# Head tiles: scaling one tile later, two output buffers, moments of the last block earlier

## The reference, cut to what matters

```python
x = x + xattn(layernorm(x), ctx, ctx)
t = layernorm(x)
scores = softmax(t @ Wg.T)                       # 8 experts
w, idx = top_k(scores, 2);  w = w / w.sum()
h1 = t @ W1[e].T + (t @ A1[e].T) @ B1[e].T + b1[e]
h3 = t @ W3[e].T + (t @ A3[e].T) @ B3[e].T + b3[e]
y_e = (silu(h1) * h3) @ W2[e].T + lora(...) + b2[e]
x = x + sum_e gates[e] * y_e
```

## Time and profile before

| | |
|---|---|
| median of the runs | 1315.3 us |
| profiled execution | 1313.04 us, of which the span is 1311.3 us |
| PE busy | 1247.3 us (95%) |
| DVE busy | 1028.2 us (78%) |
| head tiles 0 to 4 in the span | 708.77 to 776.98 us |
| tile 5 | 776.98 to 785.27 us |

### The profile page before, as it was taken

How to read it: one execution, slowest core, us unless ns; L and a number is a source line. 1 busy time by engine, 2 the same in 40 slices (tenths; PEclk the granted TensorE clock), 3 DMA queues, 4 the chain that set the end, 5 groups by cost and what they waited for, 6 DMA issues and landing times.

```text
span 1311.3 us, 34655 instructions
## 1 busy us (share of the span) xinstructions
PE 1247.3 (95%) x11734; PEld 950.9 (73%) x11734; DVE 1028.2 (78%) x3006; ACT 812.0 (62%) x1698; POOL 584.2 (45%) x742
## 2 busy tenths in 40 slices
PE   8799999999999999999998789999999999999997
PEld 6566666766667666676566568888888888888886
DVE  3779999999999999998776767767776767777664
ACT  5268777787777877778566435545555545555443
POOL 6213345554455544545316644444444443444444
PEclk9999999999999999999899889999999999999998
DMA  6678557566575664765546455555565656544444
GB/s 203 126 187 191 110 147 161 131 158 127 147 171 123 155 138 132 170 131 118 99 140 154 107 128 98 91 82 95 98 95 85 102 74 97 85 59 66 65 67 57
DMA packets 179617, 156.33 MB, mean 119 GB/s; under 512 B 105929, under 2 KB 161273, under 8 KB 175353
## 3 DMA queue, kind: packets, MB, share of 16 engines
q1 hardware_dynamic: 153586, 119.29, 41.9%
q0 software_dynamic: 25872, 35.01, 16.1%
HBM read 69.01 MB, written 66.51 MB: 103 GB/s over the span
## 4 chain that ended last, share of the span: by engine, by line
PE 84%; DMA 4%; DVE 4%; issue 4%; ACT 2%; POOL 2%; SPq 1%; POOLq 0%; ACTq 0%; DVEq 0%
PE pv_bank L836 10%; PE st_bank L820 9%; PE bank L82 8%; PE s_bank L805 8%; PE bank L83 8%; PE bank L84 8%; PE s_bank L82 4%; PE s_bank L83 4%; PE s_bank L84 4%; PE pv_bank L82 3%; PE bank L726 2%; DMA out_y<-y_out,f_token 2%; PE st_bank L83 2%; PE pv_bank L84 2%; PE st_bank L84 2%
## 5 line engine op out<-in xcount | busy, mean ns | idle before, releaser
L1060 DVE TENSOR_REDUCE maxes<-s_bank 128x2 f32<-128x512 f32 x512 | 345.8, 684 | 63.2 <-PE s_bank L805 57.2
L915 ACT ACTIVATE expo<-st_bank 128x512 f32<-128x512 f32 x512 | 300.5, 597 | 65.7 <-PE st_bank L820 63.6
L1544 POOL DMA_INDIRECT out_y<-y_out,f_token x136 | 216.4, 1591 | 25.4 <-issue 13.7
L805 PE MATMUL s_bank<-stack 65*128 65x256 bf16 x1024 | 198.6, 275 | 7.7 <-DVE maxes L1060 5.7
L820 PE MATMUL st_bank<-stack 67*128 67x256 bf16 x1024 | 198.5, 275 | 3.5 <-ACT expo L915 3.3
L1543 POOL TENSOR_TENSOR f_hold<-ones 128x1 f32<-128x1 f32 x136 | 64.3, 473 | 288.1 <-ACT y_out L1693 288.1
L1693 ACT ACTIVATE y_out<-y_sum,gate 128x256 f32<-128x256 f32 x136 | 61.7, 500 | 165.3 <-DVE y_sum L1805 149.5
L1746 DVE TENSOR_TENSOR ct_hi<-vals,ct_hi 128x256 bf16<-128x256 f32 x272 | 114.3, 421 | 43.5 <-ACT ct_hi L1664 33.9
L1664 ACT CAST ct_hi<-vals 128x256 bf16<-128x256 f32 x272 | 109.0, 401 | 62.4 <-DVE vals L1740 62.3
L1740 DVE SCALAR_TENSOR_TENSOR vals<-s_bank,b,vals 128x256 f32<-128x256 f32 x146 | 67.8, 483 | 99.3 <-ACT vals L1659 99.1
L82 PE MATMUL s_bank<-xt_hi,stack 128*128 128x256 bf16 x504 | 137.5, 273 | 7.9 <-issue 7.9
(11 more groups left out here) (236 smaller groups left out, 3073.6 us busy)
## 6 DMA issues: line engine op xcount, KB each, us to landing
stack<-qk_scratch SPq DMA_DIRECT2D x256, 128.0 KB, 4.7
qk_scratch<-qk SPq DMA_DIRECT2D x32, 512.0 KB, 3.9
x<-in_x SPq DMA_DIRECT2D x16, 512.0 KB, 7.2
ctx_in<-in_ctx SPq DMA_DIRECT2D x16, 512.0 KB, 8.0
out_y<-x SPq DMA_DIRECT2D x32, 256.0 KB, 6.5
expo<-in_w_units SPq DMA_DIRECT2D x18, 256.0 KB, 3.4
x<-in_w_units SPq DMA_DIRECT2D x18, 256.0 KB, 3.0
expert_rows<-padding SPq DMA_DIRECT2D x14, 260.0 KB, 4.5
```

The costliest lines, as they stand in the source:

```text
L805: ins = pe.matmul(s_bank[r % 2][:, n, :], stack[k][0:ROW_K, 0, h0 + n, a * P:(a + 1) * P], stack[k][0:ROW_K, 1, h0 + n, :], start=True, st ...
L915: act.activation(expo[:, s % E_RING], st_bank[s % 2][:], ACT.Exp, scale=SCALE).then_inc(exp_done, 1)
L1060: dve.tensor_reduce(maxes[:, t, h0:h0 + 2], s_bank[r % 2][:], AX_X, ALU.max).then_inc(max_done, 1)
L1544: pool.indirect_dma_start(out=dram["y"], out_offset=bass.IndirectOffsetOnAxis(ap=token[:, a:a + 1], axis=0), in_=y_out[:, a, :], in_offset ...
```

## The change

Four things in the head tiles; nothing in the attention.

- ACT scales the outputs of head tile T within tile T + 1, behind its second silu, instead of at the end of tile T. Only the last head tile scales at its own end, as later tiles do.
- `y_out` and `token` get a second buffer (the second `y_out` in a free half of `xn`); a head tile waits for the scatter of the tile two before it (`wait_scattered`), where it waited for the one just before.
- On DVE `weights_low` of a head tile goes behind the `y_sum` pair, and PE no longer waits for `sum_ready` in a head tile.
- The last block's moments and DVE's part of `scales` go from tile 1 behind the residual sum in tile 0, and ACT's two `normalize` halves one slot ahead.

The core of the diff:

```diff
--- before.py
+++ after.py
@@ -274,7 +274,7 @@
             xt=[xt[h][:].rearrange("p c t -> p (c t)").rearrange("p (n t) -> p n t", t=FT) for h in ("hi", "lo")],
             silu=vals_f[2].rearrange("p (m t) -> p m t", t=FT), act_f=vals_f[3].rearrange("p (m t) -> p m t", t=FT),
             act=[ct_hi[k][:].rearrange("p c t -> p (c t)").rearrange("p (m t) -> p m t", t=FT) for k in range(2)],
-            head_xt=head_xt, h_bank=[s_bank[0], s_bank[1], bank[0], bank[1]],
+            head_xt=head_xt, y_out_b=xn_f[:, 512:512 + FA * D].rearrange("p (n d) -> p n d", d=D), h_bank=[s_bank[0], s_bank[1], bank[0], bank[1]],
             y_bank=[pv_bank, st_bank[1]], low_bank=st_bank[0], last_use=last_use, bank_free=bank_free,
             ident=ident, ones=ones, number=number, padding=padding, tile_row=tile_row, tile_start=tile_start,
             row_end=row_end, table_ready=table_ready, row_loaded=row_loaded,
@@ -1038,8 +1038,8 @@
 
                 if (T, at) == (0, 2):
                     high(("heads", last, 1))
-                if T == 1 and at in (1, 2):
-                    normalize("r", last, at - 1)
+                if T == 1 and at in (0, 1):
+                    normalize("r", last, at)
                 if (T, at) == (1, 3):
                     high(("norm", last, 0))
                 if (T, at) == (1, 4):
@@ -1329,7 +1329,6 @@
                     low(("heads", last, 1))
                 if (T, at) == (0, 4):
                     output(("out", last, 1))
-                if (T, at) == (1, 0):
                     dve.wait_ge(*free(("out", last, 1)))
                     moments("r", last, range(2, TT), False, True)
                     scales("r", last)
@@ -1381,10 +1380,10 @@
     meta = sb("meta", [P, FA, META], F32)
     head_meta = sb("head_meta", [P, HEAD * FA, META], F32)
     y_sum = sb("y_sum", [P, FA, D], F32)
-    y_out = sb("y_out", [P, FA, D], F32)
+    y_outs = [sb("y_out", [P, FA, D], F32)[:], at["y_out_b"]]
     first_pick = sb("first_pick", [P, FA], F32)
     gate = sb("gate", [P, FA], F32)
-    token = sb("f_token", [P, FA], U32)
+    tokens = [sb(f"f_token{n}", [P, FA], U32) for n in range(2)]
     spare = sb("spare", [P, 1], U32)
     token_next = sb("token_next", [P, FA], U32)
     hold = sb("f_hold", [P, FA], F32)
@@ -1448,6 +1447,14 @@
     def meta_of(T):
         return head_meta[:, FA * T:FA * T + FA] if from_head(T) else meta[:]
 
+    def turn_of(T):
+        return T % 2 if from_head(T) else 0
+
+    def wait_scattered(engine, T):
+
+        done = max(T - 1, 0) if from_head(T) else T
+        engine.wait_ge(y_scattered, done * (16 * FA) + 16)
+
     def sync_program(sp):
 
         def pad(e, done):
@@ -1542,8 +1549,8 @@
                 pool.wait_ge(y_scaled, T * FA + FA + a + 1)
                 pool.tensor_tensor(hold[:, a:a + 1], ones[:, 0:1], ones[:, 0:1], ALU.subtract).then_inc(held, 1)
                 pool.indirect_dma_start(
-                    out=dram["y"], out_offset=bass.IndirectOffsetOnAxis(ap=token[:, a:a + 1], axis=0),
-                    in_=y_out[:, a, :], in_offset=None, compute_op=ALU.add).then_inc(y_scattered, 16)
+                    out=dram["y"], out_offset=bass.IndirectOffsetOnAxis(ap=tokens[turn_of(T)][:, a:a + 1], axis=0),
+                    in_=y_outs[turn_of(T)][:, a, :], in_offset=None, compute_op=ALU.add).then_inc(y_scattered, 16)
 
         def rest():
 
@@ -1623,8 +1630,6 @@
                 chain(T, m)
                 if m == 1:
                     update(1, T, low_bank)
-                if m == MC - 1:
-                    pe.wait_ge(sum_ready, T + 1)
 
             tile(T, 0, between)
 
@@ -1689,8 +1694,8 @@
                 act.wait_ge(y_read, T * FA + FA + a + 1)
 
                 if a == 0:
-                    act.wait_ge(y_scattered, T * (16 * FA) + 16)
-                act.activation(y_out[:, a, :], y_sum[:, a, :], ACT.Copy,
+                    wait_scattered(act, T)
+                act.activation(y_outs[turn_of(T)][:, a, :], y_sum[:, a, :], ACT.Copy,
                                scale=gate[:, a:a + 1]).then_inc(y_scaled, 1)
 
         def tile(T, e):
@@ -1701,9 +1706,15 @@
 
             if T == 0:
                 act.wait_ge(bias_loaded, 48)
-            inner(T, 0, lambda m: chain(T, m))
+            def between(m):
+                chain(T, m)
+                if m == 1 and T:
+                    outer(T - 1)
+
+            inner(T, 0, between)
             weights_high(1, T)
-            outer(T)
+            if T == HEAD - 1:
+                outer(T)
 
         def early_tile(T, e, n):
             inner(T, e)
@@ -1761,8 +1772,8 @@
 
         def keep_token(T):
 
-            dve.wait_ge(y_scattered, T * (16 * FA) + 16)
-            dve.tensor_copy(token[:], token_next[:]).then_inc(gate_ready, 1)
+            wait_scattered(dve, T)
+            dve.tensor_copy(tokens[turn_of(T)][:], token_next[:]).then_inc(gate_ready, 1)
 
         def add(e, u, bank):
 
@@ -1803,6 +1814,7 @@
             for a in range(FA):
                 dve.wait_ge(y_ready, T * FA + a + 1)
                 dve.tensor_tensor(y_sum[:, a, :], y_bank[a][:, 0, :], b2[e], ALU.add).then_inc(y_read, 1)
+            between(6)
 
         def head_tile(T, chain):
 
@@ -1811,7 +1823,7 @@
                     add(1, T, low_bank)
                 if m < 5:
                     chain(T, m)
-                if m == 5:
+                if m == 6:
                     weights_low(1, T)
 
             if T == 0:
```

## The result

Over twelve runs each the changed kernel takes 1306.88 us (1304.19 to 1309.85) and the kernel before 1313.96 (1310.47 to 1320.32; the 1315.3 above is the median of three of these). The ratio is 0.9947, with a 95% interval of 0.9932 to 0.9963: 0.53% faster, 7.0 us, between 4.9 and 8.9. The two profiled executions take 1313.04 and 1306.34, 6.7 apart.

A forecast was written before the change was run, and what follows sets the result against it. PE, full from tile 5 on, lost time in tiles 1 to 4 to waits and half clock behind them; 56.78 to 44.1 us gave 12.7, cut at tile 6 to 10.0, less 0.9 for clock: 9.1 net, 1304, range 1301 to 1310.

The forecast's parts named there:

- Tile 1, 9.8: Head tile 1, from 14.18 to 9.8 us: 8.29 clean, 0.9 for eight transposes, 0.6 waiting for product(1, 0).
- Tile 2, 11.7: Head tile 2, from 13.68 to 11.7 us: 8.29 clean, 0.8 small matmuls, 2.6 of waits with the gate's chain exposed.
- the 0.9 charged for the third product: In tile 2, the table load back to silu delays the third product, 0.9 us in two pieces.
- Tiles 3 and 4, 12.9 and 9.7: Head tiles 3 and 4, from 14.13 and 14.79: DVE-bound with 4.6 of waits; 1.44 of loop bounds, token copy's wait gone.
- Table 7.4 earlier, tile 6's load at 770.2, its rows at 775.3: Chain into tile 6: earlier table, load issued 19.05 us after it, landing in 4.6, DVE copy 0.42; PE waits 2.7.
- Half of 1.7 us charged for the clock: At tile 6, half clock behind the new 2.7 us wait was uncertain, so 0.9 us was charged.
- The low halves' place, nothing: In the head tiles, the low half's new place costs nothing, being first used in expert 1's tiles.
- the second buffers, the token copy's 3.23 us: In tile 4's sum, the token copy's 3.23 us go, since it waits for the scatter two tiles before.
- The first rival: Tile 6's rows later still: load takes 6.95 us rather than 4.6, half clock follows, 6.0 gained, 1307; 14%.
- The second: DVE bounds tiles 2 and 3, PE waits as long elsewhere, only tile 1's 4.4 us stay: 1308.7; 14%.
- Half clock through whole tiles: Slower rival: PE works in short bursts, clock at half through tiles 2 to 5, about 14 us slower, 1327; 5%.
- the rule weighed in the prediction: Skill's drain of about 1.38 us per table switch: tile 2 would lose up to 1.4 more, gain 7.7.

The follow-up runs named there:

- Experiments 3 and 5: 3: changed kernel with POOL's split of rows moved ahead of tile 0's send, 1306.36 us; 5: changed kernel with that split in two halves, 1303.76 us.
- experiment 8: Changed kernel with tile 6's load ahead of the six paddings and POOL's split of rows in two halves: 1299.31 us.
- Experiment 6: Changed kernel with the weights' low halves back ahead of the residual sums: 1305.93 us, ratio 0.9931 to the kernel before.
- Experiment 7: Changed kernel with one buffer each for scaled outputs and tokens, and the scatter waits that go with it: 1309.81 us, ratio 0.9970 to the kernel before.
- kernel 2: Changed kernel with the early moments and normalizations undone, the rest kept: 1309.20 us, ratio 0.9961 to the kernel before.
- kernel 1: Kernel before with only the early moments and normalizations of the change: 1310.50 us, ratio 0.9981 to the kernel before.
- kernel 9: Kernel before with only tile 6's load moved ahead of the padding stores of experts 2 to 7: 1313.35 us, ratio 1.0004.

## Why the prediction was right, and where it was off

The forecast, 1304 with 1301 to 1310, against 1306.88: the direction and the mechanism held. By its own steps:

- *Tile 1, 9.8.* Measured 10.13. The wait for the rows is gone, the one for product(1, 0) is 0.63 (forecast 0.6), and the clock is 1.00.
- *Tile 2, 11.7.* Measured 13.63: this is the term that failed, by 1.9. Of that, 1.55 is half clock, which the forecast put at nothing in this tile. The waits are 2.93 where 2.6 were charged, and two errors nearly cancel in them: the 0.9 charged for the third product did not come, and pick cost 1.2 more. The forecast took pick at 1.93 from a row of before in which POOL's split stood elsewhere. Moved 7 us earlier, pick met it, and its cast took 1.34 for 0.17. The prediction had read the same effect off tile 1's low half and didn't ask where POOL's instruction, which hardly moved, would stand against the instructions that were pulled forward. Experiments 3 and 5 show the cause. That the clock fell, experiment 8 shows, is not owed to the 1.2 us alone: there it fell behind 1.77. What reaches the end of these two losses is the later table; the half clock in tile 2 is hidden behind tile 6's rows.
- *Tiles 3 and 4, 12.9 and 9.7.* Measured 12.34 and 10.09. The four waits in tile 3 are 3.6 together where 4.6 were charged; tile 4 has 1.63 of issue for 1.44.
- *Table 7.4 earlier, tile 6's load at 770.2, its rows at 775.3.* Measured: the table ends at 752.38, 6.1 earlier, 1.3 later than forecast, nearly all of it the cast. From there to the load it is 19.6 us (19.05 before), and from its issue to tile 6's first matmul 4.7 (5.1 in the forecast, from a landing of 4.6 that is 4.2 here; what lands last is the second, small load, which SP issues 1.5 us behind the first). Together 776.73 instead of 775.3. The new wait is there, as forecast: 2.25 for 2.7.
- *Half of 1.7 us charged for the clock.* The whole was paid, 4.1 us at 0.59. This half and the 1.4 above are the 2.3 us between the forecast net gain of 9.1 and the measured 6.8 (tile 7 begins at 787.64 instead of 794.45).
- *The low halves' place, nothing, and the second buffers, the token copy's 3.23 us.* Experiment 6 does not contradict the first, within its wide interval. Experiment 7 gives 3.0 for the second by the ratios, with intervals that overlap, by a longer wait (4.86) and a partial return at tile 6. The scaling's own move was not undone alone: kernel 2 has it together with the buffers and the low halves' place.

The first rival (tile 6's rows later, 1307) names the number that came, but not by its mechanism: the load landed sooner than forecast, not in 6.95. That the number is the same is luck. The second, DVE as the bound, falls with tiles 1 to 4 (46.19 for 56.78). Half clock through whole tiles did not come; the longest piece in any of these kernels is 7 us, in kernel 1.

On the rule weighed in the prediction: the switch of the table takes 1.28 and the exponential starts 0.02 behind it, as in the earlier trace rows; with the switch on PE's path, no time for a drain is to be seen there, nor ahead of the switch (it starts 0.02 behind the silu, at 733.87). The Trainium skill, ScalarE: Activation LUTs, section "What ACT_TABLE_LOAD costs", would have it 1.38 longer; the measurement decides.

What stays open is when the clock falls: a wait of 1.77 us was followed by half clock in kernel 8 and not in 5, and the wait of 2.47 for the normalized rows was followed by it in the kernel before and not in kernel 9, where PE goes on at full clock (1.00 from 728.15 to 735):

```profile
728.15 0.63 PE L753 MATMUL bank<-ident,rn 128*128 128x128 f32 x4 [2.47 <-ACT rn L971]
```

Over all eleven profiles, tiles 1 to 6: the clock fell at each of the eleven waits of 2.81 us and longer, and at seven of the seventeen from 1.77 to 2.78. So half of 1.7, as the forecast charged it for a wait of 2.7, was a fair price, and that the whole came was one of its two outcomes. No experiment here controls it.

## What to carry to other kernels

When an instruction is pulled forward, ask for each engine that did not move what it will now stand beside: a cast, a copy or a subtraction of DVE beside POOL's split ended with POOL's instruction, or its own time behind it. A gain upstream ends at the first chain that was in time only by a little; look through the queue that feeds the next stage (here six paddings ahead of a load) and reorder it along with the change. A new wait on PE is best charged with the whole piece at half clock (1.7 us) from some 2.8 us on, by the count above, and with about half of it from 1.8 to 2.8; a single profile's stretch is to be read with some 3 us as its noise.

## What the runs showed of the hardware

POOL's split and some of DVE's instructions hold each other up by whole instructions. Beside POOL's cast or subtraction a cast of 8 elements on DVE took 1.34 for 0.17, a copy of 2 elements 2.09 for 0.17, a subtraction 2.19 for 0.69. The small ones ended within 0.1 us of POOL's instruction, the larger ones their own time (0.6) behind it. POOL waits in turn: its subtraction, 2.12 in the changed kernel, took 2.46 in kernel 1 and 2.36 in kernel 3, where a subtraction of DVE was still running as it began (until 732.30 and 724.78). Not all of DVE is held: FIND_INDEX8 (0.16 each, 735.92 to 736.49 in the changed kernel) and a product that reads a PSUM bank (0.48, at 724.73 in kernel 3) ran on beside the same subtraction.

The Trainium skill, SBUF — State Buffer, section "🔬 SBUF: two separate sides", says it as a rule: DVE and GpSimd share a pair of ports as an exclusive lock; a DVE instruction with two inputs in SBUF (against a GpSimd one that reads SBUF) or in a two-port mode, and a GpSimd instruction, shut each other out, and whoever starts first holds the pair for the whole instruction. The rows agree with the exclusion by whole instructions; in which mode the small cast and copy ran no row shows. On who goes first they do not all agree: kernel 1's low half starts at 730.11, ahead of POOL's cast at 730.69, and is through only 0.56 behind that cast's end. The measurement decides; why is open (POOL was issuing an indirect DMA when the low half started, 729.69 to 730.69).
